# Relation sums on rows stored as two 12-bit halves, with a ring of 24 gathered runs

## What is computed

```python
transformed = jnp.einsum('ni,rio->rno', x, W) + b[:, None, :]
msgs = transformed[edge_types, src]
agg = jnp.zeros((N_REL, num_nodes, D_OUT), x.dtype).at[edge_types, dst].add(msgs)
s = jnp.transpose(agg, (1, 0, 2))
qkv = s @ in_proj_w.T + in_proj_b
...
aggregated_output = attended.mean(axis=1)
out = (aggregated_output + x[:, :D_OUT]) @ proj_w.T + proj_b
```

## Time and profile before

| | |
|---|---|
| median of 3 runs | 6818.97 us (6811.69 to 6829.78) |
| profiled execution, span from first to last instruction | 5694.7 us |
| profiled execution, own time | not recorded beside the span |
| median less span | 1124.3 us |
| granted TensorE clock, mean | 0.962 |
| busy: TensorE, VectorE, ScalarE, GpSimd | 4877.5, 3997.7, 2701.6, 3457.0 us |

### The profile page before, as it was taken

How to read it: one execution, slowest core, us unless ns; L and a number is a source line. 1 busy time by engine, 2 the same in 40 slices (tenths; PEclk the granted TensorE clock), 3 DMA queues, 4 the chain that set the end, 5 groups by cost and what they waited for, 6 DMA issues and landing times. The chain is left out here.

```text
span 5694.7 us, 146960 instructions
## 1 busy us (share of the span) xinstructions
PE 4877.5 (86%) x41806; PEld 3603.8 (63%) x41807; DVE 3997.7 (70%) x12069; ACT 2701.6 (47%) x9241; POOL 3457.0 (61%) x3690
## 2 busy tenths in 40 slices
PE   8769988998888888867976888888888888888887
PEld 4358877887777778764534555555555556555554
DVE  6448888888888888866756666666666666666662
ACT  5446666666666666642211444434443444434344
POOL 4357777777777777763437755555565555655530
PEclk9879999999999999988988999999999999999998
DMA  6788888888888888895654544444444444444431
GB/s 204 147 248 244 253 249 249 253 251 250 252 249 251 250 251 247 241 169 152 223 187 140 154 136 126 131 134 124 140 130 126 137 131 130 136 121 128 132 93 32
DMA packets 559523, 1024.62 MB, mean 180 GB/s; under 512 B 83160, under 2 KB 345388, under 8 KB 559218
## 3 DMA queue, kind: packets, MB, share of 16 engines
q0 software_dynamic: 222096, 682.80, 42.4%
q1 hardware_dynamic: 209112, 190.72, 11.3%
q10 hardware_dynamic: 128074, 148.80, 8.9%
HBM read 883.11 MB, written 142.09 MB: 180 GB/s over the span
## 5 line engine op out<-in xcount | busy, mean ns | idle before, releaser
L1868 POOL DMA_INDIRECT rm_xg<-tx_rows,rm_src x1568 | 1492.3, 952 | 1002.8 <-PE rm_pa L1913 584.8
L936 POOL DMA_INDIRECT at_kv<-kv_rows,at_idx x1760 | 1675.3, 952 | 605.1 <-issue 477.1
L2261 DVE SCALAR_TENSOR_TENSOR rm_acc<-rm_acc,rm_kp,rm_pa 126x256 f32<-126x256 f32 x1875 | 898.4, 479 | 457.3 <-PE rm_pa L1913 340.4
L1913 PE MATMUL rm_pa<-rm_xg,rm_oh 128*126 x3750 | 1018.5, 398 | 71.4 <-ACT rm_kp L2176 36.6
L1913 PEld LDWEIGHTS rm_pa<-rm_xg,rm_oh 128*126 128x126 f32 x3750 | 656.9, 191 | 349.2 <-issue 251.4
L1044 PE MATMUL at_p_s<-at_hot,at_own 128*64 128x128 f32 x7040 | 732.4, 286 | 18.1 <-ACT at_own L1113 15.4
L1032 PE MATMUL at_p_k<-g_ident,at_kv 128*128 128x128 f32 x3520 | 482.6, 281 | 291.2 <-DMA at_kv<-kv_rows,at_idx 254.5
L1047 PE MATMUL at_p_s<-at_kt,at_own 128*64 128x128 f32 x7040 | 708.9, 279 | 0.0
L2077 ACT ACTIVATE rm_pr<-rm_psc,rm_ntop 126x126 f32<-126x126 f32 x1200 | 421.7, 364 | 590.1 <-DVE rm_ntop L2288 355.1
L1212 DVE SCALAR_TENSOR_TENSOR at_acc<-at_acc,at_fac,at_p_o 128x129 f32<-128x129 f32 x1760 | 612.4, 348 | 87.9 <-ACT at_fac L1126 38.3
L1113 ACT ACTIVATE at_own<-at_rec 128x256 f32 x1760 | 585.6, 406 | 127.6 <-issue 111.6
(11 more groups left out here) (307 smaller groups left out, 6870.4 us busy)
## 6 DMA issues: line engine op xcount, KB each, us to landing
at_row<-rows ACTq DMA_DIRECT2D x440, 128.0 KB
agg_rows<-rm_acc SPq DMA_DIRECT2D x300, 126.0 KB
rm_st<-agg_rows ACTq DMA_DIRECT2D x75, 504.0 KB
rm_srow<-agg_rows ACTq DMA_DIRECT2D x75, 504.0 KB
tx_rows<-up_tx SPq DMA_DIRECT2D x49, 768.0 KB, 3.6
at_kv<-kv_rows,at_idx POOLq DMA_INDIRECT x1760
rm_xg<-tx_rows,rm_src POOLq DMA_INDIRECT x1568
sums<-at_acc SPq DMA_DIRECT2D x196, 64.5 KB
```

The lines of the kernel that those rows point to most:

```text
L936: eng.indirect_dma_start(out=kv[j][:, c, 16:16 + KV], out_offset=None, in_=t.kv, in_offset=bass.IndirectOffsetOnAxis(ap=idx[:, o:o + 1], a ...
L1868: eng.indirect_dma_start(out=xg[:, g % XR, :], out_offset=None, in_=t.tx, in_offset=bass.IndirectOffsetOnAxis(ap=of[:, g:g + 1], axis=0),) ...
L1913: eng.matmul(p_a[q % BANKS][0:WR, 0:D], oh[:, q % OR, :], xg[:, bass.ds(at[q], 1), :].rearrange("p g c -> p (g c)"), start=True, stop=True ...
L2261: v_.scalar_tensor_tensor(acc[:, q % AR, :], acc[:, (q - 1) % AR, :], kp[0:WR, q % AR:q % AR + 1], p_a[q % BANKS][0:WR, 0:D], ALU.mult, AL ...
```

## The change

`update_phase` splits each transformed row. ScalarE copies it into a float32r tile, which rounds it to the upper half (`high_halves`); GpSimd subtracts this from the row, which leaves the lower half (`low_halves`). The two add up exactly to the float32 row. Both do this for tile i-6, the store moves from i-6 to i-7, and a row in `tx_rows` is now 512 numbers (2 KB), a tile 1.5 MB. `relate_mix_phase` gathers both halves and multiplies each by a float32r one-hot into the same bank. The ring goes from 32 to 24 slots. For room, the lists `row` and `keep` become bf16, and in the last phase `hid` shares `att`, and `y` shares `z`.

```diff
-        BANKS, XR, OR, AR, IR = 3, 32, 15, 25, 75
+        BANKS, XR, OR, AR, IR = 3, ROWS_RING, 15, 25, 75
...
-        xg = s.sb("xg", [P, XR, D])
-        oh = s.sb("oh", [P, OR, WR])
+        xg = s.sb("xg", [P, XR, 2, D])
+        oh = s.sb("oh", [P, OR, WR], F32R)
...
-                            out=xg[:, g % XR, :], out_offset=None, in_=t.tx,
+                            out=xg[:, g % XR, :, :].rearrange("p k c -> p (k c)"), out_offset=None, in_=t.tx,
...
-                    eng.matmul(p_a[q % BANKS][0:WR, 0:D], oh[:, q % OR, :],
-                               xg[:, bass.ds(at[q], 1), :].rearrange("p g c -> p (g c)"), start=True, stop=True
-                               ).then_inc(summed, 1)
+                    for half in (1, 0):
+                        mm = eng.matmul(p_a[q % BANKS][0:WR, 0:D], oh[:, q % OR, :],
+                                        xg[:, bass.ds(at[q], 1), half, :].rearrange("p g c -> p (g c)").bitcast(F32R),
+                                        start=(half == 1), stop=(half == 0))
+                    mm.then_inc(summed, 1)
...
-        TURN, TIMES, TAKE, STORE = 3, 4, 5, 6
+        TURN, TIMES, TAKE, SPLIT, STORE = 3, 4, 5, 6, 7
...
+                def low_halves(j, b):
+
+                    for m in range(3):
+                        eng.wait_ge(high_done, j * 3 + m + 1)
+                        tt(halves[b][:, 2 * m:2 * m + 2, 1, :], tx[b][:, 2 * m:2 * m + 2, :],
+                           halves[b][:, 2 * m:2 * m + 2, 0, :], ALU.subtract).then_inc(low_done, 1)
...
+                def high_halves(j, b, uses):
+
+                    for m in range(3):
+                        eng.wait_ge(tx_done, j * 3 + m + 1)
+                        if m == 0 and past(j, R):
+                            eng.wait_ge(tx_out[b], uses * 16)
+                        act(halves[b][:, 2 * m:2 * m + 2, 0, :].bitcast(F32R), tx[b][:, 2 * m:2 * m + 2, :],
+                            ACT.Copy).then_inc(high_done, 1)
...
                     eng.wait_ge(tx_ps, j * 3 + m + 1)
-                    if m == 0 and past(j, R):
-                        eng.wait_ge(tx_out[b], uses * 16)
+                    if past(j, R):
+                        eng.wait_ge(low_done, (j - R) * 3 + m + 1)
...
-        t.tx = nc.dram_tensor("tx_rows", [NB * P * R6, D], F32, kind="Internal").ap()
+        t.tx = nc.dram_tensor("tx_rows", [NB * P * R6, 2 * D], F32, kind="Internal").ap()
```

More of the change, by code:

```diff
@@ L9 @@
 F32 = mybir.dt.float32
+F32R = mybir.dt.float32r
 BF16 = mybir.dt.bfloat16
@@ L49 @@
 RING1 = 25
+ROWS_RING = 24
 ACCS = 8
@@ L106, in prepare_phase @@
         src1 = s.sb("src1", [P, G2 * P], I32)
[L107 to L108 removed]
+        row1 = s.sb("row1", [P, G1 * P], BF16)
+        keep = s.sb("keep", [P, G1 * P], BF16)
         need = s.sb("need", [P, G1 * P], U16)
@@ L1294, in update_phase @@
         xt = [s.sb(f"xt{i}", [P, 2, P]) for i in range(R)]
-        tx = [s.sb(f"tx{i}", [P, R6 * D]) for i in range(R)]
+        tx = [s.sb(f"tx{i}", [P, R6, D]) for i in range(R)]
+        halves = [s.sb(f"halves{i}", [P, R6, 2, D]) for i in range(R)]
         p_to = [s.ps(f"pto{i}", [P, 512]) for i in range(R)]
@@ L1401, in _ @@
                 affine(NB - 1, (NB - 1) % R)
+                for j in range(NB - SPLIT, NB):
+                    low_halves(j, j % R)
             @block.tensor
@@ L1494, in _ @@
                 copy_rows(NB - 1, (NB - 1) % R)
+                for j in range(NB - SPLIT, NB):
+                    high_halves(j, j % R, j // R)
             @block.vector
@@ L1685, in relate_mix_phase @@
         att = s.sb("att", [P, 2, SN])
-        hid = s.sb("hid", [P, 2, SN])
+        hid = att
         z = s.sb("z", [HH, 2, D])
@@ L2428, in resnorm_gnn @@
         t.ident_b = s.sb("ident_b", [P, P], BF16)
-        t.ones = s.sb("ones", [P, P])
         t.src_head = s.sb("src_head", [P, 50], I32)
@@ L2435, in resnorm_gnn @@
             s0 = Scope(nc, layer0, "g0")
+            t.iota_i = s0.sb("iota_i", [P, IW], I32)
+            t.ones = s0.sb("ones", [P, P])
             t.src0 = s0.sb("src0", [P, G0 * P], I32)
```

44 lines of the change are left out of this document (23 added, 21 removed).

## The result

| | before | after | ratio |
|---|---|---|---|
| median | 6815.33 us (4 runs, 6806.19 to 6829.78) | 7062.66 us (4 runs, 7049.98 to 7076.10) | 1.0354 (1.0332 to 1.0377) |
| forecast | | 6659 us, range 6510 to 6810 | 0.977 |

The change makes the kernel slower by 3.5%, 247 us, outside the range.

What follows compares the result with a forecast made beforehand. TensorE was taken to bound the update phase and the last phase. -315 + 98 + 49 + 8 = -160 us gave a span of 5535 and a time of 6659 us, range 6510 to 6810.

Steps and rivals of the forecast that it cites:

- So 1124.3 us lie around the span, and I leave them as they are.: Whole run: profiled span 5694.7 us against median 6819.0; the difference was taken as unchanged time outside the span.
- Term 1: Relate phase: two float32r matmuls replace a float32 sum, 0.25 us instead of 0.43; -315 us (-375 to 0).
- Rival C: Relate phase: a half costs as much as today's half, so sums save nothing; 6876 us, chance 0.15.
- Term 2: Relate phase: shorter sums uncover TensorE waits for share copy, accumulation and ring, 0.35 us a turn; +98 us (0 to 150).
- The granted clock: Last phase: 0.99 before; a fall was named only as a sign of being wrong, with no price.
- Term 3: Relate phase: 1600 gathers of doubled 2 KB rows stay hidden, DMA share near 0.78; no cost.
- the ring: Relate phase: 24 slots instead of 32 stall ScalarE in few turns, 0.05 us a turn, counted within the uncovered waits.
- Term 4: Update phase: ScalarE's copies lengthen the loop, so a tile goes from 6.46 to 7.6 us; +49 us (0 to 80).
- All transfers are under 7.6: Update phase: with doubled stores a tile's transfers take at most 6.5 us of the DMA engines, below the 7.6 us tile.
- inside the range: Update phase: VectorE and GpSimd excluding each other costs up to 0.8 us a tile, 35 us, within the forecast's range.
- Tail: End of update phase: six tiles of GpSimd subtractions left and a last store twice as long; +8 us.
- 0.16 for slower: Whole kernel: chance given to a slower result, beside 0.78 for faster by over 0.3% and 0.06 for no difference.

Runs made afterwards that it cites:

- c1: The whole changed kernel, unedited, run again at the lower level beside the kernel before: 5874.49 against 5698.16 us, ratio 1.0307.
- b2: Kernel before with each sum as two float32r matmuls on the same 1 KB row, no split, lower level: 5651.83 us, ratio 0.9917.
- f3: Changed kernel without GpSimd's subtractions and with the doubled store issued from ScalarE's queue: 6924.34 us, ratio 1.0143 to before.
- c4: Changed kernel without ScalarE's copies, the upper half cleared once and stored as zeros: 5817.98 us, ratio 1.0219 to before.
- f1: Kernel before with two float32r matmuls a sum on 1 KB rows, no split, at the upper level: 6877.42 us, ratio 1.0063.

## Why the prediction was wrong, point by point

- **"So 1124.3 us lie around the span, and I leave them as they are."** This failed first. The span and the times were of two levels; the time is the span and 1.7 us. Everything that was read from that profile is true of the lower level only. It is not what turned the sign: at the lower level, where the sum was -160, the change costs +176 us (c1). Of those 336 us, 214 lie in the scores' stretch of the last phase and 114 in the update tile.
- **Term 1, the sum, -315.** Right in mechanism, and nearly in size: TensorE's work at full clock fell by 293 us (b2) and 295 us (c1), and two sums take 0.47 us. Rival C, the half no cheaper, has the right sign for the wrong reason.
- **Term 2, what this uncovers, +98 (0.35 us a turn).** Right in size as TensorE's idle time, which grew by 95 us in b2 and 118 us in c1. Where it sits is in part other than told. Of 84 us more in 3400 to 5400 us of b2, 36 are issue before the mask matmuls, 21 the copy rm_gt that the prediction named, and 19 ScalarE's copy of the shares; the wait for VectorE's accumulation is 19.2 us in both. And it is not spread evenly: in the turn of c1 shown above ScalarE's queue holds the chain for over 4 us.
- **The granted clock, at nothing.** This is the step that failed in the last phase, and the larger failure: 174 of the 214 us. The prediction named a fall of the clock only as a sign of being wrong and put no price on it. The clock fell from 0.99 to 0.93 (b2) and 0.92 (c1), and that took 145 and 174 us back (the estimate of the table). With it the forecast of -217 for the phase becomes the -3 that c1 has: -295 + 174 + 118.
- **Term 3, the gathers, nothing.** Right for the ring (1.0004), and with long sums. With short sums 50 us; the lead-in, paced by gathers, costs 18 more. The DMA share was 0.75 (forecast 0.78), and that was no bound.
- **Term 4, the update tile, 7.6 us, +49.** It came to 9.94 us and +163, twice the upper end of its own range. GpSimd's subtraction was priced right (1.35, measured 1.325 us), the copies too (0.6, 0.62). A loop with the copies in it was to take 7.5 us, and with the copies in place, the subtraction gone and the store moved the tile is 6.97 (f3); the copies do cost 1.28 us where the rest is there (c4). What was missed is an order that the diff shows: the doubled store, which now also waits for GpSimd, stands ahead of the next tile's loads in SyncE's queue (0.97 to 1.65 us). "All transfers are under 7.6" asked for bandwidth and not for order. The loads then land late in every second tile, TensorE waits, and the clock falls there too: the short tile, of 7.8 us, is close to the forecast, which may be chance, and the long one, of 13, is not in it. The stretch of VectorE was put at 0.8 us and "inside the range"; with GpSimd's own time the subtraction costs 1.3 to 2.0.
- **Tail, +8.** 5 us behind the last xb: right.
- **The chances.** 0.16 for slower was too little. Nearly all of it was given to a half that is no cheaper, and none to a longer tile or to the clock.

At the upper level 247 us are +163 (update phase) and about 5 (its tail); the rest, some 80 us, is the last phase with its lead-in, where b2's half of the change alone costs about 50 (f1). That split isn't measured, since before has no profile there. What sets the level stays open.

## What to carry to other kernels

Compare the span of a profile with the times before anything else: if they differ by more than a few microseconds, they are two executions at different levels, and a second profile is worth more than a sum. When a transfer grows or its wait is moved to a later producer, list what is queued behind it on that engine; here taking one store out of the loads' queue is worth 1.0 to 1.65 us a tile. Price by kind of turn and tile, not in the mean: a mean tile of 9.94 us was one of 7.8 and one of 13. And where a saving leaves TensorE idle more often, put a price on its clock: here it took back half or more of what the shorter sums gave.
